# A transposed layer norm inside a two-layer attention kernel: the same norm over tokens instead of over an averaging product

## The reference, cut to what matters

```
def shift_token(t):                       # the upper 64 features come from the token before
    t1, t2 = jnp.split(t, 2, axis=-1)
    t2 = jnp.pad(t2, ((0, 0), (1, 0), (0, 0)))[:, :-1]
    return jnp.concatenate([t1, t2], axis=-1)

o = local_attention(q, k, v)              # 8 heads of 64, windows of 64 tokens
x = x + o @ wo                            # output projection, 512 -> 128
h = shift_token(x)
mu = h.mean(-1, keepdims=True)            # over the 128 features of a token
var = h.var(-1, keepdims=True)
h = (h - mu) / jnp.sqrt(var + 1e-05) * lg + lb
h = h @ w1 + b1
a, g = jnp.split(h, 2, axis=-1)
h = a * jax.nn.gelu(g, approximate=False)
x = x + h @ w2 + b2
```

## Time and profile before

| | |
|---|---|
| median of three runs | 1315.2 us |
| lowest, highest | 1311.35, 1317.98 us |
| the profiled execution, its own time | 1315.5 us |
| its span, first to last instruction | 1313.7 us |
| TensorE matmuls busy | 1264.7 us (96%) |
| ScalarE busy | 1162.1 us (88%) |
| GpSimd busy | 1147.3 us (87%) |
| VectorE busy | 1088.4 us (83%) |
| the chain that ended last | TensorE 75%, GpSimd 7%, ScalarE 6%, VectorE 5% |

### The profile page before, as it was taken

How to read it: one execution, slowest core, us unless ns; L and a number is a source line. 1 busy time by engine, 2 the same in 40 slices (tenths; PEclk the granted TensorE clock), 3 DMA queues, 4 the chain that set the end, 5 groups by cost and what they waited for, 6 DMA issues and landing times.

```text
span 1313.7 us, 38163 instructions
## 1 busy us (share of the span) xinstructions
PE 1264.7 (96%) x13793; PEld 1011.5 (77%) x13794; DVE 1088.4 (83%) x1883; ACT 1162.1 (88%) x3529; POOL 1147.3 (87%) x840
## 2 busy tenths in 40 slices
PE   7889999999999999899988999999999999999998
PEld 4777888888888887566657788888888888876776
DVE  6788888888888887599877888899988898983777
ACT  4778999999999998787768899999999999998886
POOL 4888999999999998399778999999999999984776
PEclk9999999999999999999998999999999999999999
DMA  5122222222222221011011222221112222110223
GB/s 165 35 74 62 62 62 66 66 62 62 62 70 70 58 50 38 17 32 38 1 29 30 46 46 46 50 50 46 46 46 47 51 52 50 38 39 25 66 79 97
DMA packets 60298, 70.04 MB, mean 53 GB/s; under 512 B 8912, under 2 KB 38288, under 8 KB 60112
## 3 DMA queue, kind: packets, MB, share of 16 engines
q1 hardware_dynamic: 60112, 67.61, 20.5%
HBM read 13.33 MB, written 4.19 MB: 13 GB/s over the span
## 4 chain that ended last, share of the span: by engine, by line
PE 75%; POOL 7%; ACT 6%; DVE 5%; issue 4%; DMA 2%; SPq 1%; ACTq 0%; DVEq 0%; POOLq 0%
PE ps L203 59%; PE ps L268 8%; PE ps L278 3%; PE ps L281 3%; POOL t L1259 3%; ACT P L655 3%; POOL hxr L1259 2%; DVE t L975 1%; POOL P L1259 1%; DMA norm<-X 1%; DVE nm L1006 1%; DVE t L987 1%; ACT sqk L629 1%; DVE sums L994 1%; POOL side L1289 1%
## 5 line engine op out<-in xcount | busy, mean ns | idle before, releaser
L655 ACT ACTIVATE P<-ps,nm 128x128 f32<-128x128 f32 x1024 | 364.2, 384 | 4.2 <-DVE nm L1006 4.1
L203 PE MATMUL ps<-wqkv,hT 128*128 128x512 f32 x1152 | 330.7, 429 | 14.4 <-DVE t L975 10.4
L1259 POOL TENSOR_TENSOR t<-t 128x1024 f32<-128x1024 f32 x128 | 307.5, 2402 | 32.8 <-DVE t L975 30.4
L1259 POOL TENSOR_TENSOR P<-P,rden 128x512 f32<-128x512 f32 x256 | 294.6, 1160 | 31.0 <-DVE rden L1013 28.9
L203 PEld LDWEIGHTS ps<-wqkv,hT 128*128 128x128 f32 x1152 | 217.0, 190 | 92.0 <-issue 28.4
L1259 POOL TENSOR_TENSOR t<-t,rr 128x1024 f32<-128x1024 f32 x128 | 244.0, 1906 | 19.7 <-ACT rr L638 19.3
L655 ACT ACTIVATION_READ_ACCUMULATOR P<-ps,nm 128x1 f32 x1024 | 230.1, 225 | 0.0
L987 DVE TENSOR_TENSOR t<-ps,tabl 128x512 f32<-128x512 f32 x256 | 164.1, 683 | 41.0 <-ACT sqk L629 39.3
L1259 POOL TENSOR_TENSOR hxr<-hxf,hxr 128x512 fp32r<-128x512 f32 (+1 forms) x93 | 130.8, 1434 | 67.9 <-ACT hxr L711 67.8
L1006 DVE TENSOR_REDUCE nm<-ps 128x4 f32<-128x512 f32 x256 | 173.4, 679 | 6.4 <-PE ps L203 6.3
L645 ACT ACTIVATE PT<-ps 128x1024 f32<-128x1024 f32 x128 | 130.5, 1019 | 48.2 <-PE ps L268 47.3
(11 more groups left out here) (140 smaller groups left out, 2548.5 us busy)
## 6 DMA issues: line engine op xcount, KB each, us to landing
Vs<-Vn SPq DMA_DIRECT2D x224, 128.0 KB, 2.3
side<-in_x SPq DMA_DIRECT2D x17, 256.0 KB, 2.9
A<-X SPq DMA_DIRECT2D x16, 256.0 KB, 2.5
norm<-X SPq DMA_DIRECT2D x32, 128.0 KB, 2.2
norm<-X SPq DMA_DIRECT2D x32, 127.8 KB, 2.4
hsh<-X SPq DMA_DIRECT2D x31, 128.0 KB, 2.3
hsh<-X SPq DMA_DIRECT2D x31, 127.8 KB, 2.3
oT<-in_x SPq DMA_DIRECT2D x15, 256.0 KB, 2.9
```

Of the source, the lines that this page charges most:

```text
L203: return e.matmul(o, lhsT, rhs, start=start, stop=stop, skip_group_check=True)
L655: k = act(P[:, g, :], ps[:, 3 + s, (g % 4) * 128:(g % 4 + 1) * 128], ACT.Exp, bias=nm[:, g:g + 1], accum_out=den[:, g:g + 1])
L1259: return e.tensor_tensor(o, a, b_, op)
```

## The change

The norm is done with tokens on the partitions. When the shifted residual `h2` of a sequence has landed, TensorE transposes it tile by tile into PSUM (`turn_h`, four transposes, step 4b+8). VectorE takes the statistics of each token straight from PSUM (`stats_h`, step 4b+9, 4 bn_stats and 4 bn_aggr), ScalarE makes 4 reciprocal roots per partition (`root_h`, two small operations, step 4b+9), VectorE subtracts and scales with two per-token scalars (`apply_h`, 4 operations of 128 columns, at the end of step 4b+9) into `hn0`, TensorE transposes back (`turn_back`, four transposes, step 4b+10) and ScalarE copies the result to `B` (`keep_h`, step 4b+11). The two averaging products, the subtraction, the square, the logarithm and exponential over 128x512 and the multiplication go. The output projection is one group of four products of 512 columns in step 4b+7, where there were two groups of 256 columns in steps 4b+5 and 4b+7, with one addition on VectorE. The input's statistics in layer 0 move one step earlier, to step 4b+8, with a second buffer for their result.

Bank 2 is held by the turned residual from `turn_h` until `apply_h` has read it, so `rec_out` of layer 1 now waits for `apply_h` of the sequence before.

```diff
-            def proj(l, b, u, bank):
+            def proj(l, b):
+                m = l * NB + b
+                e.wait_ge(s_o, l * NT + 4 * b + 4)
+                if b:
+                    e.wait_ge(s_hn, m)
...
                 for c in range(4):
-                    k = mm(ps[:, bank, 0:256], wo[:, l, c, :], oT[:, c, u * 256:u * 256 + 256], c == 0, c == 3)
+                    k = mm(ps[:, 2, :], wo[:, l, c, :], oT[:, c, :], c == 0, c == 3)
                 k.then_inc(s_wo, 1)
-            def mean(l, b, bank):
-                e.wait_ge(s_h2, 32 * (l * NB + b + 1))
-                mm(ps[:, bank, :], avg, h2[:]).then_inc(s_mu, 1)
-
-            def var(l, b, bank):
-                e.wait_ge(s_sqh, l * NB + b + 1)
-                mm(ps[:, bank, :], avg, rsd[:]).then_inc(s_va, 1)
+            def turn_h(l, b):
+                m, bank = l * NB + b, turn_bank(l, b)
+                e.wait_ge(s_h2, 32 * (m + 1))
+                if l == 0 and b + 3 < NB:
+                    e.wait_ge(s_x, b + 4)
+                for t in range(TPB):
+                    k = e.transpose(ps[:, bank, t * 128:(t + 1) * 128], h2[:, t * 128:(t + 1) * 128], idf[:])
+                k.then_inc(s_nt, 1)
+
+            def turn_back(l, b):
+                m, bank = l * NB + b, back_bank(b)
+                e.wait_ge(s_na, m + 1)
+                if l and b + 1 < NB:
+                    e.wait_ge(s_osq, b + 2)
+                for t in range(TPB):
+                    k = e.transpose(ps[:, bank, t * 128:(t + 1) * 128], hn0[:, t * 128:(t + 1) * 128], idf[:])
+                k.then_inc(s_nu, 1)
...
             def rec_out(b, bank):
                 e.wait_ge(s_hs, b + 1)
+                if b:
+                    e.wait_ge(s_na, NB + b)
+                else:
+                    e.wait_ge(s_b1g, 2)
...
-            def log_var(l, b, bank):
-            def root_var(l, b):
-            def square_hc(l, b):
+            def root_h(l, b):
+                m = l * NB + b
+                e.wait_ge(s_ns, m + 1)
+                act(nrs, nmv[:, :, 1], ACT.Ln, bias=eps_ln).then_inc(s_nr0, 1)
+                e.wait_ge(s_nr0, m + 1)
+                act(nrs, nrs, ACT.Exp, scale=-0.5).then_inc(s_nr, 1)
+
+            def keep_h(l, b):
+                e.wait_ge(s_nu, l * NB + b + 1)
+                if l:
+                    e.wait_ge(s_hs, b + 1)
+                act(seq(B, b), ps[:, back_bank(b), :], ACT.Copy).then_inc(s_hn, 1)
...
-            def centre(l, b, bank):
-            def scale_hc(l, b):
+            def stats_h(l, b):
+                m, x = l * NB + b, ps[:, turn_bank(l, b), :]
+                e.wait_ge(s_nt, m + 1)
+                for t in range(TPB):
+                    k = e.bn_stats(nst[:, t, :], x[:, t * 128:(t + 1) * 128])
+                k.then_inc(s_nb, 1)
+                e.wait_ge(s_nb, m + 1)
+                for t in range(TPB):
+                    k = e.bn_aggr(nmv[:, t, :], nst[:, t, :])
+                k.then_inc(s_ns, 1)
+
+            def apply_h(l, b):
+                m, x = l * NB + b, ps[:, turn_bank(l, b), :]
+                e.wait_ge(s_nr, m + 1)
+                if m:
+                    e.wait_ge(s_nu, m)
+                for t in range(TPB):
+                    k = ts(hn0[:, t * 128:(t + 1) * 128], x[:, t * 128:(t + 1) * 128], nmv[:, t, 0:1], nrs[:, t:t + 1],
+                           ALU.subtract, ALU.mult)
+                k.then_inc(s_na, 1)
...
                     if b == 1:
-                        square_hc(l, NB - 1)
+                        e.preload_act_table_set(ATTN)
+                        root_h(l, NB - 1)
+                        e.preload_act_table_set(MIXED)
                     if b < NB:
                         gelu(l, b, 2)
...
                     if b == 1:
-                        e.preload_act_table_set(ATTN)
-                        log_var(l, NB - 1, 7)
-                        root_var(l, NB - 1)
-                        e.preload_act_table_set(MIXED)
+                        keep_h(l, NB - 1)
```

More of the change, by code:

```diff
@@ L69, in program @@
         norm = sb("norm", [128, 3 * L])
-        h2, sq, rsd = (norm[:, j * L:(j + 1) * L] for j in range(3))
+        h2, hn0 = (norm[:, j * L:(j + 1) * L] for j in range(2))
         hsh = sb("hsh", [128, 2, L])
@@ L95, in program @@
         cw = [cols[:, 4 + j:5 + j] for j in range(4)]
-        one, eps_ln, eps_rms, ln2x8, mln2, part = (cst[:, i:i + 1] for i in range(6))
-        avg = part.to_broadcast([128, 128])
+        one, eps_ln, eps_rms, ln2x8, mln2 = (cst[:, i:i + 1] for i in range(5))
         ax, ez, u, dd, lnu, ru, half, nx, mx = (ab[:, i:i + 1] for i in range(9))
@@ L778, in scalar @@
                         norm_rt(l, i - 1)
+                    if (b := hit(i, 9)) is not None:
+                        root_h(l, b)
                     if i == 0:
@@ L1170, in vector @@
                     if l == 0:
[L1171 to L1173 removed]
+                        for b in due(i, -8, {0: -1, 1: -1, 2: STATS[2]}):
                             ln_stats(b)
@@ L1192, in vector @@
                         row_max(l, i - 2, 1)
-                    if l and (b := hit(i, 5)) is not None:
-                        proj_add(l, b, 0, 2)
                     if i == 1:
@@ L1201, in vector @@
                         row_max(l, 0, 1)
+                    if (b := hit(i, 9)) is not None:
+                        apply_h(l, b)
                     if l == 0 and i == STATS[1]:
```

183 lines of the change are left out of this document (62 added, 121 removed).

## The result

| | before | after |
|---|---|---|
| median | 1314.31 us (4 runs, 1311.35 to 1317.98) | 1377.84 us (4 runs, 1376.87 to 1378.61) |
| ratio to before | | 1.0482 [1.0453, 1.051] |
| profiled execution, its span | 1313.7 us | 1376.4 us |
| TensorE matmuls busy | 1264.7 us (96%) | 1260.8 us (92%) |
| ScalarE, GpSimd, VectorE busy | 88, 87, 83% | 83, 82, 80% |

The kernel is 4.8% slower. On another chip the same file gave 1374.43 us against 1315.64 for before, 1.0433 [1.0402, 1.0464].

What follows compares the result with a forecast made beforehand. The prediction took each attention step to be bound at about 7.2 us by a loop through several engines, not by TensorE's total work. 1315.5 + 22 (layer 0) + 41 (layer 1) - 4 (feed-forward) = 1374 us, own range 1350 to 1392.

Steps and rivals of the forecast that it cites:

- The floor of a step: Attention stages: each step costs about 7.2 us through a loop over several engines; only extras above 0.9 us count.
- The rival in which TensorE's saved work comes off everywhere: TensorE keeps its bound, short and long steps average out, 27 us less work gives 1289 us; chance 0.12.
- +1.74 into the 0-step: Projection work moved to the end of the 3-step (step number modulo 4) lengthens the distance behind it by 1.74 us.
- the calculation by columns: TensorE product time goes with columns: 0.217 us for 256, 0.435 for 512, so the wide projection saves nothing.
- the rival of the cheap wide product: Products of 512 columns cost less per column, 0.6 in place of 1.74 us per sequence, giving 1340 us; chance 0.08.
- -0.3 into the 2-step of layer 0: Distance losing the half projection regains only 0.3 us, held by GpSimd's last normalisation; ends 0 and 0.8.
- The total of layer 0: Attention stage of layer 0: +1.74 - 0.3 = 1.44 us per sequence, times 15, +22 us.
- times 15: Each attention stage's loss per sequence was multiplied by 15 sequences, taken from one regular period.
- Layer 1: Attention stage: +1.74, and +1.0 from the recurrence's product waiting for bank 2, per sequence, times 15, +41 us.
- The feed-forward stages: Last sequence's norm runs there with two tiny ScalarE operations for two passes: -2 us per layer, -4 in all.
- The clock rival: TensorE's clock falls to half in layer 1's thinner 1-step, 1.7 us in each of 15 sequences, 1400 us; chance 0.12.
- The cancelling rival: Layer 1's wait is covered and layer 0 regains 0.8 us; with a better feed-forward stage about 1318 us; chance 0.06.

Runs made afterwards that it cites:

- the second trial: Changed kernel with VectorE's statistics and subtract-and-scale of layer 0's last sequence moved earlier in the feed-forward stage; 1375.05 us, 1.0438 of before.
- the split projection: Changed kernel with subtract-and-scale before the sums of squares and, in layer 0, the projection's first 256 columns in the 2-step; 1385.76 us, 1.052 of before.

## Why the prediction came out right, step by step

**The floor of a step** (7.2 us whatever TensorE has to do) held: the distances that lost a product of 0.87 us and got transposes of 0.45 are 7.19 to 7.34. The rival in which TensorE's saved work comes off everywhere, 1289 us, is refuted by these and by the kernel with all turns doubled. What stands behind the floor was only partly right. In the kernel before 7.14 of the 7.19 us are TensorE's own work, and ScalarE holds 0.05. In the changed kernel TensorE has 6.7 us of work there, and the step stayed at 7.2 in layer 0 even without ScalarE's row sums, with TensorE waiting for VectorE's copy of k or GpSimd's P; the prediction named ScalarE's loop alone.

**+1.74 into the 0-step**: 1.71 in layer 0 (8.45 to 10.16), 1.64 in layer 1 (8.11 to 9.75). The step before is the projection's and nothing covers it. The trace bears out the calculation by columns: from the wide projection to the transposes of q, 889.12 - 886.09 and on to 891.63, pass 5.54 us; before, with half of it, 3.82; the difference is 1.72. With that the rival of the cheap wide product, 1340, is out, and the kernel with two narrow groups at the same place, no slower and no faster, says the same.

**-0.3 into the 2-step of layer 0**: 8.01 to 7.75, right as a number, but not by the mechanism named, GpSimd's last normalisation. In the kernel before 8.01 is TensorE's own work, 7.14 - 0.86 + 1.73. In the changed kernel TensorE waits in that step for VectorE: 0.81 us for the rotation in front of the products of q and k, and 0.31 in front of the mask products, which start 0.1 us behind the copy of k; the copy stands behind the subtract-and-scale in VectorE's list. GpSimd's P is waited for by no row there. The kernel with the projection alone has the first wait (0.96) and not the second, and 7.51. That the new norm fell near the 0.3 named is luck.

**The total of layer 0**, 22 us, was sized too high: +14.2. By the regular period alone it would be 15 x 1.6 = 24. The step that was wrong is "times 15": before does not have fifteen periods of 30.84. Its first has 36.79 us and after's 33.34 (one step there took 12.29 us in before, with a wait of 1.97 us and behind it the stretch at half clock of the earlier trace rows, and 7.72 in after): 5.0 less than forecast. The second period gives 1.2 less, the later ones 2.9, since before has 30.9 to 31.7 in six of them while after has 32.44 nearly throughout, and the steps at the two ends 0.6: 24.0 - 9.7 = 14.3. The largest among the later ones, twice 0.83 us, have a cause that the trace shows. VectorE and GpSimd in before, in such a period:

```profile
423.77 2.23 DVE L1045 TENSOR_TENSOR B<-norm 128x512 f32<-128x512 f32 x1
```

```profile
423.41 2.04 POOL L1259 TENSOR_TENSOR P<-P,rden 128x512 f32<-128x512 f32 x2
```

and in a usual one:

```profile
300.01 1.22 DVE L1045 TENSOR_TENSOR B<-norm 128x512 f32<-128x512 f32 x1
```

```profile
299.64 2.49 POOL L1259 TENSOR_TENSOR P<-P,rden 128x512 f32<-128x512 f32 x2
```

The multiplication takes 0.66 us where it starts ahead of GpSimd's half of P, which then takes 1.40 in place of 1.04 (in all regular periods of layer 0 in the kernel with the projection alone; starts 305.78 and 305.95), 1.22 when GpSimd is in the middle of one half of P, with GpSimd's next half at 1.5 in place of 1.04, and 2.2 when it has to let both halves pass. In the two periods with 2.2 the next distance is 8.03 and 8.05, in the other regular ones 7.2 to 7.6. Without the row sums ten periods of layer 0 have it, with 2.27, and each shows a distance of 8.1 or 8.2: so layer 0 became 2.8 us longer there (495.0 to 497.8), while layer 1, where the multiplication took 1.15 us at most, became 4.0 shorter. The change takes this instruction away, a small gain that the prediction had not seen. The Trainium skill, SBUF — State Buffer, "Who interferes with whom", says that a VectorE instruction with two SBUF inputs contends with a GpSimd instruction that reads SBUF, for a lock that one of them holds; the page's summary for kernel authors says that the second to issue blocks fully until the first finishes. The traces agree with 0.66 and 1.22 us. The 2.2 goes beyond it: the multiplication started at 423.77 and also let a half of P pass that began only at 424.41. I did not run a kernel that changes this overlap alone.

**Layer 1**: +41 forecast, +42.7 measured. The mechanism is the one forecast, product with A behind the subtract-and-scale: TensorE waited 1.65 us there (some 1.5 had been named), and into the 2-step it is +1.38 for +1.0. The term was undersized by 0.4 in two places: with PSUM as source the four operations take 1.36 us where the same reading gave 1.11 in the earlier trace rows, 401 to 412 ns each against 343, and the product with A starts 0.15 behind their end. They began 4.56 us behind the transposes of P, a little sooner than the 4.66 of the forecast. The period is 3.03 longer and not 2.74, which times 15 is 45.5; that the total is near 41 is in part luck, since the first distance of the layer was 11.14 in before, partly at half clock, and is 7.95 now. The early order of the same four operations took 1.34 off the distance, so the cause is shown; it is worth 14.5 of the 22.6 us by which layer 1 is slower than with the projection alone.

**The feed-forward stages**: -4 forecast, +5.5 measured, the step that failed. The prediction counted only VectorE's wait for GpSimd and let two small operations take the place of two long ones. Three things were missing. First, "times 15" leaves out the sixteenth sequence: its whole projection now stands behind the last transposes of P, in this stage. In layer 0 it passes in 3.43 us there (552.70 to 556.13) where half of it passed in 1.72 (537.01 to 538.73). That is 1.7 us in each layer, and most of the 2.3 and 2.9 us that the kernel with the projection alone is slower in these stretches; in its layer 0 the rest are two waits, each 0.3 longer. Second, a new owner of bank 6: the turned residual sits where the down projection must go until statistics, roots and scaling are through, a wait of 3.36 us for 1.47, and the second trial shows 1.8 us of it. Third, the clock, at half in two stretches of layer 0's stage where before had none.

Counted from the last transposes of P, the changed kernel starts the first down projection 4.7 us later than before, the second 6.6 later, and ends the stage 5.3 later; 1.3 us come back behind the second. Where they come back I have not taken apart, nor how the last stretch of the kernel, with the same 1.7 us more of projection, came out even.

**The total**: 1374 against 1377.8 is closer than its parts. Layer 0 came out 8 us below its forecast, layer 1 at 2 above, the feed-forward stages at 9.5 above; that the first and the last nearly cancel is luck.

**The clock rival**, 1400, did not come in the regular periods of the attention stages: a step of layer 1 with gaps of 0.95 and 1.65 us kept 1.00. The clock fell in places not thought of, above all in the feed-forward stage of layer 0, with 3.0 and 5.9 us of TensorE work at half (546.6 to 550.0 and 567.1 to 573.9). That costs at most half of it, 4.5. In the second run of the same kernel the fall behind the gap lasted 3.4 us and not 6.8, so this part differs from run to run.

**The cancelling rival**, 1318, would have needed the hand-over of bank 2 to be covered; even the early order leaves 8.94 us in that distance.

## What to carry to other kernels

Where steps of a pipeline have a floor set by a loop through several engines, sum the excess over the floor step by step: work moved from a step with slack to a full one costs its whole length, and work removed below the floor is worth nothing. The floor itself can be held by several engines at once, so making one of them faster may not move it. Before moving an operand into PSUM, list who else needs that bank until its last reader is done and where that reader stands in its engine's list; of the experiments here that moved a wait, the split projection and the move to bank 7 met the next tenant of a bank, and the recurrence's product moved behind V met GpSimd's P. And count the periods of a trace before multiplying by one of them, the one at the end too, which may fall into another stage.

## What was not expected of the hardware

- A VectorE multiplication with both inputs in SBUF took 0.66, 1.22 or 2.2 us, by how it fell against GpSimd's operations, and slowed these in turn (two halves of P in 2.49 for 2.04 us, one half in 1.40 for 1.04).
- Subtract-and-scale of 128x128 float32 with per-token scalars took 343 ns from SBUF and 401 to 412 ns from PSUM.
- Eight extra float32 transposes of 128x128 per period were free in steps under the floor but for 0.1 us in one place, and the granted clock stayed at 1.00 over them in the regular periods.
